# Pair attention in fp32: TensorE runs the first layer of two steps in a row, then two steps of scores

## The chip, the cores and the metric

The kernel runs on one core of a Trainium2 chip. The metric is the device time of one execution in microseconds (us), lower being better. Three executions of the kernel before gave 1324.63, 1326.22 and 1329.87 us, a median of 1326.22 us.

## What is computed

The reference takes x of shape 2048 x 40 x 64 (samples, fields, embedding). For every sample it forms all 780 products of two different fields, sends each through a small net (64 to 64, relu, 64 to 1), makes a softmax over the 780 logits and pools the products with it. All is fp32.

```
p = x[:, ROW, :]
q = x[:, COL, :]
inner = p * q
h = jax.nn.relu(jnp.einsum('bpe,he->bph', inner, W1) + b1)
logits = jnp.einsum('bph,oh->bpo', h, W2) + b2
attn = jax.nn.softmax(logits, axis=1)
pooled = jnp.sum(inner * attn, axis=1)
return pooled @ Wl.T + bl
```

## The kernel before

The samples are taken as two halves, whose embeddings lie above each other on the 128 partitions; a sample of the one half with its partner of the other is a "duo". One step (t) treats 2 duos, a round (r) is 16 steps, and 32 rounds make the whole. Each engine has its own program, and they meet in semaphores; there is no scheduler, so the order on an engine is the order in which its code calls the helpers.

One step goes through four engines' programs like this:

- VectorE (`products`, L463) multiplies fields pairwise into `inner`, a ring of 8 steps. Two steps share one small tail instruction (L482), after the odd step.
- TensorE (`hidden_layer`, L285) multiplies by W1. It does so in two halves, each into its own PSUM buffer (`h_bank[0]`, `h_bank[1]`), with 64x64 tiles of the array, so that four matmuls run at once (two row tiles, two column tiles). There is no second pair of such buffers: before it writes half 0 it waits until ScalarE has read half 0 of the step before (`hidden_ready`, L292), and the same for half 1. Half 0 also waits for the products.
- ScalarE (`relu`, L405) reads one half from PSUM, adds the bias, applies relu and writes `hidden`, a ring of 4 steps. Before step t it waits until step t-4 has been scored.
- TensorE (`score`, L303) multiplies `hidden` by w2 with 128x32 tiles, four at once, and adds 16 steps of a round into one of two logit banks. It waits for both relu halves of its step.

Between these, TensorE has other work that is not in every step: `turn_chunk` (L255, five transposes of new input, in steps 0 and 8 of a round) and `gram_matrix` (L266, sixteen small matmuls with 128x40 operands, in steps 4, 6, 12 and 14). Below, both are called fillers. ScalarE copies the results out of PSUM: `copy_turned` in steps 0, 0, 2, 3 and 8, 9, 11, 11 (parts 0 and 1 are the copies to `xt`, parts 2 and 3 those to `x_scaled`), and `copy_gram` in steps 5, 6, 13 and 15, always behind the two relus of that step. In step 3 it also computes the exponentials of the round before (`exp_of_round`). VectorE takes the maximum of the round before in step 7 of its own program (`softmax_of_round`, L488), after a wait for the last scores of that round, and its sums in step 8 (L500). In round 0 the places of chunk 1 are one step later, and round 31 has no work for a next round.

The order on TensorE is written in `round_steps` (L322): first layer of step t, scores of step t-1, then a filler if the step has one. The last scores of a round come in step 0 of the next.

Of the kernel before, what the change touches and what calls it, by code (L numbers as in the profile page):

```python
# [19 lines left out]
def pair_attention_kernel(nc, x, w1, b1, w2, b2, wl, bl, y):  # L20
# [17 lines left out]
    WINDOWS = 16  # L38
# [29 lines left out]
    with ExitStack() as ctx:  # L68
# [3 lines left out]
        def pb(name, shape):  # L72
            return ctx.enter_context(nc.psum_tensor(name, shape, F32))
# [44 lines left out]
        logit_bank = [pb(f"logit_bank{n}", [P, BANK]) for n in range(2)]  # L118
# [135 lines left out]
        def _(pe):  # L254
            def turn_chunk(r, c):  # L255

                pe.wait_ge(x_loaded[c], 32 * (r + 1))
                if not (r == 0 and c == 0):

                    pe.wait_ge(gram_copied, 2 * (r * CHUNKS_PER_ROUND + c))  # L260
                for t in range(TT):
                    last = nc.tensor.transpose(turn_bank[:, t * P:(t + 1) * P],  # L262
                                               x_rows[c][:, t, :, :].rearrange("p h e -> p (h e)"), ident[:, :])
                last.then_inc(turned, 1)

            def gram_matrix(r, c, part):  # L266

                pe.wait_ge(scaled_ready, 2 * (r * CHUNKS_PER_ROUND + c + 1))
                if not (r == 0 and c == 0 and part == 0):

                    pe.wait_ge(gram_copied, 2 * (r * CHUNKS_PER_ROUND + c) + part)
                for n in range(GRAM_DUOS):
                    duo = part * GRAM_DUOS + n
                    for half in range(2):
                        scaled_at = (2 * duo + half) * GRAM_COLUMNS
                        fields_at = duo * EXT + half * SPAN
                        last = nc.tensor.matmul(  # L277
                            turn_bank[half * TILE:half * TILE + GRAM_COLUMNS,
                                      GRAM_AT_COLUMN + n * FIELDS:GRAM_AT_COLUMN + (n + 1) * FIELDS],
                            x_scaled[:, scaled_at:scaled_at + GRAM_COLUMNS],  # L280
                            xt[c][:, fields_at:fields_at + FIELDS], start=True, stop=True,
                            tile_position=(0, half * TILE))
                last.then_inc(gram_ready, 1)

            def hidden_layer(r, t):  # L285
                for half in range(2):
                    if half == 0:

                        pe.wait_ge(inner_ready, inner_to(r, t))
                    if not (r == 0 and t == 0):  # L290

                        pe.wait_ge(hidden_ready, (r * WINDOWS + t) * 2 + half - 1)  # L292
                    for ab in range(2):
                        rows = slice(ab * EMBED, (ab + 1) * EMBED)
                        for j in range(STEP_DUOS):
                            at = (t % INNER_RING) * STEP + j * PAIRS + half * HALF
                            last = nc.tensor.matmul(  # L297
                                h_bank[half][j * TILE:(j + 1) * TILE, ab * BANK:ab * BANK + HALF],
                                w1_block[rows, rows], inner[rows, at:at + HALF], start=True, stop=True,
                                tile_position=(ab * TILE, j * TILE))  # L300
                    last.then_inc(h_ready, 1)

            def score(r, t, bank):  # L303

                pe.wait_ge(hidden_ready, (r * WINDOWS + t + 1) * STEP_DUOS)
                if t == 0 and r == 0:
                    pe.wait_ge(w2_loaded, 2 * 16)
                first = WINDOWS - 1 - t  # L310
                for half in range(2):
                    for ab in range(2):
                        g = 2 * half + ab
                        at = half * PAIRS + ab * HALF
                        last = nc.tensor.matmul(bank[g * QUAD:(g + 1) * QUAD, 0:HALF],  # L315
                                                w2_window[:, first:first + QUAD],
                                                hidden[t % RING][:, at:at + HALF],
                                                start=(t == 0), stop=(t == WINDOWS - 1),
                                                tile_position=(0, g * QUAD))
                last.then_inc(steps_scored, 1)  # L320

            def round_steps(r, odd, first=False, last=False):  # L322
                for t in range(WINDOWS):
                    hidden_layer(r, t)
                    if t:
                        score(r, t - 1, logit_bank[odd])
                    elif not first:
                        score(r - 1, WINDOWS - 1, logit_bank[1 - odd])
                    if first and t == 0:
                        gram_matrix(r, 0, 1)  # L330
                    for part in range(2):
                        if t == GRAM_AT[1][part] + first:
                            gram_matrix(r, 1, part)
                        if t == GRAM_AT[0][part] and not last:
                            gram_matrix(r + 1, 0, part)
                    if t == TURN_AT[1] + first:
                        turn_chunk(r, 1)
                    if t == TURN_AT[0] and not last:
                        turn_chunk(r + 1, 0)
# [7 lines left out]
            pe.wait_ge(w1_ready, 1)  # L347
            gram_matrix(0, 0, 0)
            round_steps(0, 0, first=True)
            for pair in range(ROUNDS // 2 - 1):  # L350
                round_steps(2 * pair + 1, 1)
                round_steps(2 * pair + 2, 0)
# [239 lines left out]
```

## Time and profile before

| | before |
|---|---|
| median of three executions | 1326.22 us |
| the profiled execution | 1324.93 us |
| its span (first to last instruction) | 1323.3 us |
| TensorE (PE) busy | 1306.2 us, 99% |
| ScalarE (ACT) busy | 1093.5 us, 83% |
| VectorE (DVE) busy | 1006.5 us, 76% |
| mean granted TensorE clock | 0.998 |

The rows of the trace further down are of this one execution. PE are TensorE's matmuls and PEld its weight loads. The ends of matmul records are modelled and overlap, so the pace of TensorE is read from the starts. An fp32 matmul of the program shows as two records.

### The profile page before, as it was taken

The page shows a single profiled execution, that of the slowest core. Times are in us where ns is not written, and L with a number is a line of the kernel's source. Part 1 is how long each engine was busy: PE and PEld are TensorE (multiplying, and loading weights), DVE is VectorE, ACT ScalarE, POOL GpSimd, SP SyncE. Part 2 cuts the span into 40 slices and gives each one's busy share as a digit, 9 for nine tenths or more (in the row PEclk, how much of TensorE's full clock was granted, in tenths as well). Part 3 has the DMA queues.
Part 4 walks back from the last instruction along what each step waited for, and adds up shares of the span by engine and source line. Part 5 has one row for each costly group of instructions (what it writes and reads, how often), then busy time and mean ns, then how long its engine had stood idle before and what let it go on. Part 6 is the DMA issues. An engine that isn't in the chain of part 4 may idle for free.

```text
span 1323.3 us, 38688 instructions
## 1 busy us (share of the span) xinstructions
PE 1306.2 (99%) x16709; PEld 463.4 (35%) x16709; DVE 1006.5 (76%) x1613; ACT 1093.5 (83%) x1475; POOL 0.7 (0%) x6
## 2 busy tenths in 40 slices
PE   7999999999999999999999999999999999999997
PEld 3333333333333333333333333333333333333332
DVE  8688777887777877778877778777787777887774
ACT  6888888888888888888888888888888888888885
POOL 0000000000000000000000000000000000000000
PEclk9999999999999999999999999999999999999999
DMA  2211211212112112111121121211211211112100
GB/s 48 47 36 40 47 24 40 47 30 47 37 28 46 34 44 47 21 43 38 39 46 24 41 46 30 47 42 23 46 34 43 46 22 43 36 40 46 24 21 20
DMA packets 176792, 49.73 MB, mean 38 GB/s; under 512 B 172528, under 2 KB 172528, under 8 KB 176624
## 3 DMA queue, kind: packets, MB, share of 16 engines
q1 hardware_dynamic: 176624, 47.26, 16.3%
q8 instruction: 133, 2.18, 0.7%
q14 instruction: 35, 0.29, 0.1%
HBM read 34.11 MB, written 13.12 MB: 36 GB/s over the span
## 4 chain that ended last, share of the span: by engine, by line
PE 98%; DVE 1%; ACT 0%; DMA 0%; issue 0%; SPq 0%; ACTq 0%
PE h_bank L297 57%; PE logit_bank L315 31%; PE turn_bank L277 7%; PE turn_bank L262 3%; DVE inner L474 0%; DMA x_rows<-in_r_x 0%; ACT hidden L410 0%; ACT xt L378 0%; DVE weighted L505 0%; ACT weight L418 0%; SPq L184 0%; PE turn_bank L359 0%; DVE row_max L491 0%; DVE part L564 0%; DVE inverse L568 0%
## 5 line engine op out<-in xcount | busy, mean ns | idle before, releaser
L410 ACT ACTIVATE hidden<-h_bank,b_col 128x780 f32<-128x780 f32 x1024 | 877.9, 909 | 178.2 <-PE h_bank L297 176.5
L474 DVE TENSOR_TENSOR inner<-xt 128x760 f32<-128x760 f32 x1024 | 908.5, 945 | 106.4 <-ACT xt L378 69.5
L297 PE MATMUL h_bank<-inner,w_block 64*64 64x390 f32 x8192 | 793.1, 501 | 0.7 <-DVE inner L482 0.7
L315 PE MATMUL logit_bank<-hidden,w_window 128*32 128x390 f32 x4096 | 441.8, 503 | 0.4 <-ACT hidden L410 0.4
L297 PEld LDWEIGHTS h_bank<-inner,w_block 64*64 64x64 f32 x8192 | 258.3, 132 | 409.3 <-ACT hidden L410 126.3
L315 PEld LDWEIGHTS logit_bank<-hidden,w_window 128*32 128x32 f32 x4096 | 80.7, 108 | 312.0 <-issue 310.9
L505 DVE CUSTOM_DVE_ANT_1 weighted<-weight,gram 128x380 f32<-128x380 f32 x32 | 27.7, 867 | 152.7 <-ACT weight L418 152.7
L277 PEld LDWEIGHTS turn_bank<-xt,x_scaled 128*40 128x40 f32 x4096 | 89.7, 123 | 84.2 <-issue 44.9
L277 PE MATMUL turn_bank<-xt,x_scaled 128*40 128x40 f32 x4096 | 104.9, 209 | 2.6 <-ACT x_scaled L390 2.6
L390 ACT ACTIVATE x_scaled<-turn_bank,wl_col 64x640 f32<-64x640 f32 x128 | 100.6, 786 | 1.6
L378 ACT COPY xt<-turn_bank 128x640 f32<-128x640 f32 (+1 forms) x128 | 68.3, 560 | 25.5 <-PE turn_bank L262 25.5
L401 ACT COPY gram_rows<-turn_bank 128x320 f32<-128x320 f32 x128 | 54.6, 426 | 14.5 <-PE turn_bank L277 14.5
L482 DVE TENSOR_TENSOR inner<-xt 128x80 f32<-128x80 f32 x256 | 60.2, 235 | 0.0
L491 DVE TENSOR_REDUCE row_max<-logit_bank 128x1 f32<-128x390 f32 x32 | 18.1, 564 | 49.0 <-PE logit_bank L315 49.0
L262 PE MATMUL turn_bank<-ident,x_rows 128*128 128x128 f32 x320 | 49.5, 286 | 4.6 <-DMA x_rows<-in_r_x 4.6
L262 PEld LDWEIGHTS turn_bank<-ident,x_rows 128*128 128x128 f32 x320 | 34.1, 141 | 44.6 <-issue 44.6
L418 ACT ACTIVATE weight<-logit_bank,exp_bias 128x390 f32<-128x390 f32 x32 | 18.8, 588 | 2.1 <-DVE exp_bias L497 2.1
L513 DVE CUSTOM_DVE_ANT_0 weighted<-weight,gram 64x10 f32<-64x10 f32 x64 | 10.8, 169 | 1.0
L493 DVE TENSOR_SCALAR round_stats<-row_max,b_col 128x1 f32<-128x1 f32 x32 | 6.9, 214 | 1.1
L497 DVE TENSOR_SCALAR exp_bias<-round_stats,b_col 128x1 f32<-128x1 f32 x32 | 6.8, 214 | 1.1
L418 ACT ACTIVATION_READ_ACCUMULATOR weight<-logit_bank,exp_bias 128x1 f32 x32 | 6.7, 209 | 0.0
L519 DVE COPY stats<-round_stats 128x4 f32<-128x4 f32 x32 | 5.5, 172 | 1.1
(28 smaller groups left out, 16.7 us busy)
## 6 DMA issues: line engine op xcount, KB each, us to landing
x_rows<-in_r_x SPq DMA_DIRECT2D x128, 160.0 KB, 3.4
gram_dram<-gram_rows SPq DMA_DIRECT2D x512, 25.0 KB
gram<-gram_dram SPq DMA_DIRECT2D x32, 400.0 KB, 3.3
w_rows<-in_L_rec_W SPq DMA_DIRECT2D x2, 16.0 KB, 2.3
wl_col<-in_L_rec_Wl SPq DMA_DIRECT2D x2, 0.2 KB, 2.3
b_col<-in_L_rec_b SPq DMA_DIRECT2D x2, 0.2 KB, 2.3
w_window<-in_L_rec_W SPq DMA_DIRECT2D x2, 0.2 KB, 2.3
b_col<-in_L_rec_b SPq DMA_DIRECT2D x1, 0.5 KB, 2.7
```

Source lines behind the costliest of these rows:

```text
L262: last = nc.tensor.transpose(turn_bank[:, t * P:(t + 1) * P], x_rows[c][:, t, :, :].rearrange("p h e -> p (h e)"), ident[:, :])
L277: last = nc.tensor.matmul(turn_bank[half * TILE:half * TILE + GRAM_COLUMNS, GRAM_AT_COLUMN + n * FIELDS:GRAM_AT_COLUMN + (n + 1) * FIELDS] ...
L297: last = nc.tensor.matmul(h_bank[half][j * TILE:(j + 1) * TILE, ab * BANK:ab * BANK + HALF], w1_block[rows, rows], inner[rows, at:at + HAL ...
L315: last = nc.tensor.matmul(bank[g * QUAD:(g + 1) * QUAD, 0:HALF], w2_window[:, first:first + QUAD], hidden[t % RING][:, at:at + HALF], star ...
L378: nc.scalar.copy(window_view(xt[c], at, [[EXT, CHUNK_DUOS], [TT, u], [1, TT]]), window_view(turn_bank, 0, [[U, CHUNK_DUOS], [1, u], [P, TT ...
L390: nc.scalar.activation(window_view(x_scaled, ab * SPAN, [[GRAM_COLUMNS, 2 * CHUNK_DUOS], [TT, U // 2], [1, TT]], rows), window_view(turn_b ...
L401: nc.scalar.copy(gram_rows[c][:, part * GRAM_DUOS:(part + 1) * GRAM_DUOS, :], turn_bank[:, GRAM_AT_COLUMN:GRAM_END].rearrange("p (d n) -> ...
L410: nc.scalar.activation(hidden[t % RING][:, half * PAIRS:(half + 1) * PAIRS].rearrange("p (a n) -> p a n", a=2), h_bank[half][:, :].rearran ...
L418: nc.scalar.activation(weight[:, :], bank[:, 0:HALF], ACT.Exp, bias=exp_bias[:, 0:1], accum_out=round_stats[:, 1:2]).then_inc(exp_done, 1)
L474: nc.vector.tensor_tensor(window_view(inner, to + half * HALF, [[PAIRS, STEP_DUOS], [SPAN, SHIFTS], [1, SPAN]]), window_view(xt[c], at + h ...
L482: nc.vector.tensor_tensor(window_view(inner, to + SHIFTS * SPAN, [[PAIRS, duos], [HALF, 2], [1, LAST]]), window_view(xt[c], at, [[EXT, duo ...
L505: nc.vector.tensor_tensor_reduce(out=weighted[:, 0:main].rearrange("p (d i) -> p d i", i=SPAN), in0=weight[:, 0:main].rearrange("p (d i) - ...
```

## The change

Only TensorE's order is changed. In an even step it runs the first layer (and the filler, if there is one) and no scores. In an odd step it runs the first layer and then the scores of the two preceding steps. The last step of a round is scored in step 1 of the next round, ahead of step 0. The last score of the whole kernel stays where it was.

```diff
             def round_steps(r, odd, first=False, last=False):
                 for t in range(WINDOWS):
                     hidden_layer(r, t)
-                    if t:
+                    if t % 2:
+
+                        if t > 1:
+                            score(r, t - 2, logit_bank[odd])
+                        elif not first:
+                            score(r - 1, WINDOWS - 1, logit_bank[1 - odd])
                         score(r, t - 1, logit_bank[odd])
-                    elif not first:
-                        score(r - 1, WINDOWS - 1, logit_bank[1 - odd])
                     if first and t == 0:
                         gram_matrix(r, 0, 1)
```

The next rows are TensorE's order of the kernel before in steps 2 to 5 of a round other than the first. L297 is the first layer (4 matmuls are one half of a step, the number of `h_bank` is the half), L315 is the scores, with the slot of the `hidden` ring that tells the step.

```order
L297 MATMUL h_bank0<-inner,w1_block 64x390 x4
L297 MATMUL h_bank1<-inner,w1_block 64x390 x4
L315 MATMUL logit_bank1<-hidden1,w2_window 32x390 x4
L297 MATMUL h_bank0<-inner,w1_block 64x390 x4
L297 MATMUL h_bank1<-inner,w1_block 64x390 x4
L315 MATMUL logit_bank1<-hidden2,w2_window 32x390 x4
L297 MATMUL h_bank0<-inner,w1_block 64x390 x4
L297 MATMUL h_bank1<-inner,w1_block 64x390 x4
L315 MATMUL logit_bank1<-hidden3,w2_window 32x390 x4
L277 MATMUL turn_bank<-xt1,x_scaled 40x40 x16
L297 MATMUL h_bank0<-inner,w1_block 64x390 x4
L297 MATMUL h_bank1<-inner,w1_block 64x390 x4
```

The same work in the changed kernel (an equal stretch, of a round with the other logit bank and chunk):

```order
L297 MATMUL h_bank0<-inner,w1_block 64x390 x4
L297 MATMUL h_bank1<-inner,w1_block 64x390 x4
L297 MATMUL h_bank0<-inner,w1_block 64x390 x4
L297 MATMUL h_bank1<-inner,w1_block 64x390 x4
L315 MATMUL logit_bank0<-hidden1,w2_window 32x390 x4
L315 MATMUL logit_bank0<-hidden2,w2_window 32x390 x4
L297 MATMUL h_bank0<-inner,w1_block 64x390 x4
L297 MATMUL h_bank1<-inner,w1_block 64x390 x4
L277 MATMUL turn_bank<-xt0,x_scaled 40x40 x16
L297 MATMUL h_bank0<-inner,w1_block 64x390 x4
L297 MATMUL h_bank1<-inner,w1_block 64x390 x4
L315 MATMUL logit_bank0<-hidden3,w2_window 32x390 x4
```

What moved: four halves of the first layer now follow each other where no filler stands, and a filler now stands between two first layers and no longer behind scores. The programs of the other engines are unchanged.

## Rows read from the trace of the kernel before

**Rows 1.** The page: busy time of the engines, and the chain that ended last, by engine.

```profile
PE 1306.2 (99%) x16709; PEld 463.4 (35%) x16709; DVE 1006.5 (76%) x1613; ACT 1093.5 (83%) x1475; POOL 0.7 (0%) x6
...
PE 98%; DVE 1%; ACT 0%; DMA 0%; issue 0%; SPq 0%; ACTq 0%
```

**Rows 2.** Timeline, TensorE: the six groups of four matmuls of one step (start, length).

```profile
609.86 0.56 PE L297 MATMUL h_bank<-inner,w_block 64*64 64x390 f32 x4
610.24 0.51 PE L297 MATMUL h_bank<-inner,w_block 64*64 64x390 f32 x4
610.57 0.51 PE L297 MATMUL h_bank<-inner,w_block 64*64 64x390 f32 x4
610.90 0.51 PE L297 MATMUL h_bank<-inner,w_block 64*64 64x390 f32 x4
611.34 0.54 PE L315 MATMUL logit_bank<-hidden,w_window 128*32 128x390 f32 x4
611.69 0.51 PE L315 MATMUL logit_bank<-hidden,w_window 128*32 128x390 f32 x4
```

**Rows 3.** Timeline, ScalarE, step 11, then 2 to 4: start, length, work [idle before].

```profile
610.88 1.72 ACT L410 ACTIVATE hidden<-h_bank,b_col 128x780 f32<-128x780 f32 x2 [0.55 <-PE h_bank L297]
612.48 1.60 ACT L390 ACTIVATE x_scaled<-turn_bank,wl_col 64x640 f32<-64x640 f32 x2
...
628.99 1.71 ACT L410 ACTIVATE hidden<-h_bank,b_col 128x780 f32<-128x780 f32 x2 [0.54 <-PE h_bank L297]
630.59 0.78 ACT L390 ACTIVATE x_scaled<-turn_bank,wl_col 64x640 f32<-64x640 f32 x1
631.27 1.70 ACT L410 ACTIVATE hidden<-h_bank,b_col 128x780 f32<-128x780 f32 x2
632.86 0.59 ACT L418 ACTIVATE weight<-logit_bank,exp_bias 128x390 f32<-128x390 f32 x1
...
633.56 0.79 ACT L390 ACTIVATE x_scaled<-turn_bank,wl_col 64x640 f32<-64x640 f32 x1
634.38 1.71 ACT L410 ACTIVATE hidden<-h_bank,b_col 128x780 f32<-128x780 f32 x2
```

**Rows 4.** Stretches (steps 2-3, 4-5, a round): length; busy PE, PEld, DVE, ACT, POOL; clock.

```profile
627.98:632.51 4.53, 4.53 (x53) 1.34 (x49) 0.70 (x1) 3.99 (x6) 0.00 (x0) 1.00 0.33 74
632.51:637.78 5.27, 5.27 (x84) 1.96 (x81) 4.14 (x12) 4.78 (x8) 0.00 (x0) 1.00 0.01 3
602.37:643.05 40.68, 40.68 (x526) 14.42 (x522) 31.30 (x51) 34.10 (x47) 0.00 (x0) 1.00 0.17 38
```

**Rows 5.** Timeline: where TensorE waited for a relu, in step 13 and at the end.

```profile
614.10 1.72 ACT L410 ACTIVATE hidden<-h_bank,b_col 128x780 f32<-128x780 f32 x2
...
615.87 0.21 PEld L297 LDWEIGHTS h_bank<-inner,w_block 64*64 64x64 f32 x8 [0.50 <-ACT hidden L410]
...
1311.36 1.71 ACT L410 ACTIVATE hidden<-h_bank,b_col 128x780 f32<-128x780 f32 x2 [0.55 <-PE h_bank L297]
...
1313.12 0.86 PE L315 MATMUL logit_bank<-hidden,w_window 128*32 128x390 f32 x8 [0.44 <-ACT hidden L410]
```

**Rows 6.** Timeline, TensorE: a gram and a turn, each with the first layer behind it.

```profile
599.37 0.81 PE L277 MATMUL turn_bank<-xt,x_scaled 128*40 128x40 f32 x32
...
600.11 1.54 PE L297 MATMUL h_bank<-inner,w_block 64*64 64x390 f32 x16
...
604.64 0.76 PE L262 MATMUL turn_bank<-ident,x_rows 128*128 128x128 f32 x5
...
605.33 1.54 PE L297 MATMUL h_bank<-inner,w_block 64*64 64x390 f32 x16
```

**Rows 7.** Timeline, VectorE: the softmax and the sums of one round.

```profile
625.15 0.56 DVE L491 TENSOR_REDUCE row_max<-logit_bank 128x1 f32<-128x390 f32 x1 [1.09 <-PE logit_bank L315]
...
633.57 0.87 DVE L505 CUSTOM_DVE_ANT_1 weighted<-weight,gram 128x380 f32<-128x380 f32 x1 [4.89 <-ACT weight L418]
```

**Rows 8.** Timeline, TensorE: the first layer of the kernel's first step.

```profile
10.75 2.88 PE L297 MATMUL h_bank<-inner,w_block 64*64 64x390 f32 x16 [0.68 <-DVE inner L482]
```

## The prediction

> **What bounds the kernel now.** I read the page first: TensorE is busy for 99% of the span, and 98% of the chain that ended last is TensorE's own work [rows 1]. So only TensorE's order and its waits can set the time. ScalarE has idle time, but it hands back the PSUM buffers, and must be followed step by step.
>
> Next I read TensorE's pace inside a step from the starts of its groups of four matmuls [rows 2]. They come 0.38, 0.33 and 0.33 us apart inside the first layer, 0.44 from the last one of it to the first of the scores, 0.35 inside the scores, and 0.44 from there to the next step, as two steps in 4.53 us [rows 4] tell: 4.53/2 less the 1.83 between the first and last start of the step. The bare pace is thus 0.33. A change between first layer and scores, which use different tile shapes, costs 0.11 more, and the group after it 0.02 to 0.05 more. That is the price which this change saves.
>
> Then the two clocks of a step. With the start of a first layer as zero, ScalarE's first relu starts at 1.01 (628.99 against 627.98) and the two take 1.71 together, so they end at 1.92 and 2.72 (one takes 0.91, the second starts 0.80 after the first) [rows 3, 4]. Where TensorE really waited for a relu, its next work began 0.05 behind the relu's end: 1313.12 after 1311.36 + 1.71, and 615.87 after 614.10 + 1.72 [rows 5]. Today the scores (0.79) stand in that interval and hide it nearly everywhere.
>
> **Steps 2-3 and 10-11 (no filler).** Here the next first layer could follow at 1.04 + 0.33 = 1.37, but half 0 of the PSUM buffer is read until 1.92. With its two waits it starts at about 2.0, and its second group 0.38 later, as after any fresh start. Half 1 needs the second relu: 2.72 + 0.05 = 2.78 with rounding. Then 0.38 to its second group (3.16), 0.44 to the scores (3.60). The scores of two steps are four groups, 0.35 + 0.33 + 0.33 + 0.44 = 1.45 to the next first layer. The pair takes 5.05 us instead of 4.53 [rows 4]: **0.52 more**. Of the two changes of shape saved here, one only makes the wait longer, and the other is lost in it.
>
> **Steps with a filler between.** In the pairs 0-1, 4-5, 6-7, 8-9, 12-13 and 14-15 the turn or gram, which stood behind scores, now stands between the two first layers. The trace has no filler behind a first layer. The nearest rows are the changes to another shape on either side of scores, 0.44 both, so I take 0.44: filler at 1.48. A gram holds TensorE for 0.74 until the next first layer and a turn for 0.69 [rows 6], so that starts at 2.22 or 2.17. The first relu was done at 1.92 and the second (2.72 + 0.05) is wanted at 2.22 + 0.71 = 2.93: the filler hides both waits. What remains is the gain: scores of two steps cost 1.45 in one run and 2 x 0.79 = 1.58 apart, **0.13 less**. The join of two score runs is the unknown. Its bounds are the 0.33 of an undisturbed join and the 0.44 of a change of shape [rows 2]; it is the same shape on the same bank, with weights that change at every group anyway, so I take 0.33. At 0.35 it would add 0.02 x 256 pairs = 5 us.
>
> Here a rule speaks. The Trainium skill (TensorEngine Tiling, Key Properties) says that a change of tiling mode drains the array, and its page TensorE: Matmul & The Clock Gate (Step-by-step) gives a drain as about 128 cycles, 0.05 us at 2.4 GHz as an estimate. The rows show 0.11, twice that. By the page's figure, half of the 0.11 would be something else that could stay with the join of two runs of scores, at 0.39; this is a rival below.
>
> **Where ScalarE comes late.** Its copies now meet relus that come in other intervals. In pair 2-3, after the relus of step 2, `x_scaled` starts at 1.01 + 1.60 = 2.61, the relus of step 3 at +0.82 = 3.43, the exponentials 1.59 later (5.02), the second `x_scaled` at 5.72, and the relus of step 4 at 6.54 [rows 3]. They end at 7.45 and 8.25. TensorE starts step 4 at 5.05, wants the gram at 6.53 (its input is there at about 6.6), and step 5 at 7.34, which waits until about 7.56; half 1 comes at 8.30. With 0.38 + 0.44 + 1.45 behind it pair 4-5 takes 5.51 where 5.27 stood [rows 4]: **0.24 more**. In pair 10-11 the relus of step 11 start at 3.03 and two `x_scaled` 1.60 behind that, for 1.60 [rows 3], until 6.21. The relus of step 12 end at about 7.14 and 7.94, half 1 of step 13 wants 7.98 and gets 7.99: pair 12-13 saves only **0.06**. After steps 0 and 8 the copies to `xt` push relus by 0.3, but the next first layer has more slack than that (its relu ends at 4.4, wanted at 5.1).
>
> **Costed at nothing.** The relu ring: step t waits for the scores of step t-4, and these are still done a pair earlier. VectorE takes the round's maximum about 2 us later, since the last scores of a round now follow step 1; but it then waits 4.89 us for the exponentials anyway [rows 7], and these stand on ScalarE behind step 3, some 4 us after the later maximum. The DMAs wait for turns and gram copies, a round ahead of their use. Before the first step of a pair, its products: VectorE is busy 76% [rows 1] and loses nothing.
>
> **Sum.** Per round: 2 x 0.52 - 4 x 0.13 + 0.24 - 0.06 = 0.70 us, so 41.4 instead of 40.68. Thirty such rounds: 21.0. Round 0 has fillers one step later, so four plain pairs (2, 4, 6, 10), one pair unchanged and three filled: 4 x 0.52 - 2 x 0.13 - 0.06 = 1.8. Round 31 has no fillers in its second half: 4 x 0.52 + 0.24 - 2 x 0.13 = 2.1, and the last pair, whose final scores follow without the 0.44 us wait of [rows 5], saves 0.1, so 2.0. In all 24.8 us. The profiled execution took 1324.93, which gives 1349.7; it lies 1.3 below the median of 1326.22, against which I forecast **1351.0 us**, 1.9% slower. A measurement of this kernel tells 0.5% (6.6 us) from no change.
>
> **Rivals.**
> - ScalarE comes late in one more filled pair per round, as in pair 4-5. That costs 0.37 x 32 = 12, so 1363 us. For it: ScalarE is busy 83%, and in pair 12-13 the margin is nil. Chance 0.10.
> - The join of two score runs costs 0.39: 0.06 x 256 = 15, so 1366 us. Against it: the other joins of one shape show 0.33. Chance 0.04.
> - The waits are worse than hidden. If fillers did not cover the relus, 192 filled pairs would cost 0.65 more each, so 1476 us. Or the clock drops: in the first step of the kernel, at 1.2 GHz, a first layer is 2.88 us long [rows 8] against 1.54 at 2.4 GHz [rows 6]; if the eight groups after each of 64 waits went at that pace, 2.7 us each, that is 1524 us. Against it: the wait is near 0.7 us, and after the one of 0.44 at the end TensorE goes on at full pace. Together 0.04. The Trainium skill (TensorE: Matmul & The Clock Gate, A second HAM failure mode) describes such clock swings from short idle times between groups; no idle of this kind is in the trace before.
> - **Faster.** The fillers leave the array cheaper behind a first layer than behind scores, on both sides: 0.11 less before and 0.11 less after. That is 192 x 0.22 = 42 us, so 1309 us. It decides from 0.13 per filled pair on, where 192 pairs make up for the 24.8. For it: nothing in the trace shows a filler behind a first layer. Against it: the changes that it does show, into scores and out of them, cost 0.44 alike, and a filler's tiles are of another shape than a first layer's, too. Chance 0.05.
> - Nearly no change: only one of these two sides is cheaper, 192 x 0.11 = 21, so 1330 us. Chance 0.07.
>
> **How the numbers follow.** My forecast has 0.70. Its own bounds: joins at 0.35 add 5; waits in pair 4-5 and after the relus that cost nothing extra take off 8 to 13. The range of 1338 to 1363 holds this and the first rival, 0.80 in all. Slower by over 0.5%: 0.70 + 0.10 + 0.04 + 0.04 = 0.88; within: 0.07; faster: 0.05.
>
> **What would show it.** In the profile after, TensorE's idle time in front of a first layer should be named as a wait for ScalarE's relus, some 0.6 us in each of two pairs per round, with a round of about 41.4 us. Scores should come in runs of four groups, 0.35, 0.33, 0.33 apart. Pairs 0-1, 6-7, 8-9 and 14-15 should be 0.13 shorter than before and plain ones 0.5 longer. It is wrong if filled pairs gain more than 0.13 or plain ones lose less than 0.4, or if VectorE's products become what a first layer waits for.

## The result and the profile after

| | before | after |
|---|---|---|
| median of four executions | 1325.45 us | 1344.55 us (1344.09 to 1344.99) |
| the profiled execution | 1324.93 us | 1344.98 us |
| its span | 1323.3 us | 1343.4 us |
| TensorE busy | 1306.2 us, 99% | 1285.1 us, 96% |
| ScalarE busy | 1093.5 us, 83% | 1079.8 us, 80% |
| mean granted TensorE clock | 0.998 | 0.998 |

The changed kernel is slower by 1.4%: the ratio of its runs to those of before is 1.0143, 95% interval 1.0128 to 1.0158. The forecast was 1351.0 us, in a range from 1338 to 1363. The direction and the mechanism were right; the loss is 19 to 20 us where 24.8 were worked out.

From the page after, the busy times and the chain that ended last (for [rows 1]):

```profile
PE 1285.1 (96%) x16709; PEld 482.9 (36%) x16709; DVE 1006.3 (75%) x1613; ACT 1079.8 (80%) x1475; POOL 0.7 (0%) x6
...
PE 80%; ACT 12%; DVE 5%; issue 2%; DMA 0%; ACTq 0%; SPq 0%; DVEq 0%
```

TensorE is busy 21 us less by its records (the saved changes of shape are part of that) and yet ends 20 us later. The chain, which was 98% TensorE, now has a part through ScalarE (12%, mostly its relus) and VectorE (5%; what that name is worth is told below).

The stretches of one round after, two steps each, then the whole round (columns as in [rows 4]: length, busy PE, PEld, DVE, ACT, POOL, granted clock, DMA share, GB/s). The order is steps 0-1, 2-3, and so on:

```profile
426.81:431.89 5.08, 5.08 (x57) 1.92 (x53) 1.16 (x3) 4.19 (x7) 0.00 (x0) 1.00 0.29 53
431.89:436.94 5.05, 4.52 (x53) 1.38 (x49) 2.20 (x5) 4.20 (x7) 0.00 (x0) 1.00 0.24 55
436.94:442.32 5.38, 5.26 (x85) 2.07 (x81) 4.77 (x12) 4.98 (x8) 0.00 (x0) 1.00 0.00 2
442.32:447.45 5.13, 5.13 (x84) 2.13 (x80) 5.13 (x8) 3.80 (x6) 0.00 (x0) 1.00 0.10 19
447.45:452.54 5.09, 5.09 (x57) 1.92 (x53) 4.05 (x7) 4.07 (x6) 0.00 (x0) 1.00 0.45 116
452.54:457.58 5.04, 4.51 (x52) 1.38 (x48) 4.86 (x7) 3.83 (x6) 0.00 (x0) 1.00 0.26 59
457.58:462.87 5.29, 5.26 (x84) 2.07 (x81) 5.29 (x8) 4.89 (x7) 0.00 (x0) 1.00 0.00 0
462.87:468.01 5.14, 5.14 (x85) 2.14 (x81) 3.85 (x6) 3.68 (x6) 0.00 (x0) 1.00 0.01 3
426.81:468.01 41.20, 40.00 (x527) 15.02 (x523) 31.31 (x51) 33.65 (x47) 0.00 (x0) 1.00 0.17 38
```

Two stretches of before that the prediction's rows do not show, pairs 0-1 and 12-13 of a round:

```profile
419.34:424.56 5.22, 5.22 (x57) 1.86 (x53) 3.40 (x8) 4.64 (x8) 0.00 (x0) 1.00 0.23 39
449.40:454.75 5.35, 5.35 (x85) 1.96 (x81) 5.35 (x8) 4.95 (x7) 0.00 (x0) 1.00 0.00 0
```

The plain pairs, those without a filler (second and sixth row after), are 5.04 to 5.05 us long with 0.53 us in which TensorE does nothing by its records; before they had 4.53 and no idle time. Pairs 0-1 and 8-9 have gone from 5.22 to 5.09, pairs 6-7 and 14-15 from 5.27 to 5.13. Pair 4-5 has gone from 5.27 to 5.38, pair 12-13 from 5.35 to 5.29. A round is 41.20 instead of 40.68.

The timeline of a plain pair and the step after it, TensorE and ScalarE alone (for [rows 3]; start, length, work, idle before it and what ended it):

```profile
596.72 1.54 PE L297 MATMUL h_bank<-inner,w_block 64*64 64x390 f32 x16
...
597.73 1.71 ACT L413 ACTIVATE hidden<-h_bank,b_col 128x780 f32<-128x780 f32 x2 [0.85 <-PE h_bank L297]
598.75 0.24 PEld L297 LDWEIGHTS h_bank<-inner,w_block 64*64 64x64 f32 x8 [1.18 <-DVE inner L477]
598.78 1.60 PE L297 MATMUL h_bank<-inner,w_block 64*64 64x390 f32 x16 [0.53 <-ACT hidden L413]
599.33 0.78 ACT L393 ACTIVATE x_scaled<-turn_bank,wl_col 64x640 f32<-64x640 f32 x1
599.49 0.21 PEld L297 LDWEIGHTS h_bank<-inner,w_block 64*64 64x64 f32 x8 [0.50 <-ACT hidden L413]
600.01 1.70 ACT L413 ACTIVATE hidden<-h_bank,b_col 128x780 f32<-128x780 f32 x2
...
600.31 1.52 PE L315 MATMUL logit_bank<-hidden,w_window 128*32 128x390 f32 x16
...
601.76 1.54 PE L297 MATMUL h_bank<-inner,w_block 64*64 64x390 f32 x16
...
602.29 0.79 ACT L393 ACTIVATE x_scaled<-turn_bank,wl_col 64x640 f32<-64x640 f32 x1
...
603.11 1.72 ACT L413 ACTIVATE hidden<-h_bank,b_col 128x780 f32<-128x780 f32 x2
```

The second first layer starts at 598.78, that is 2.06 behind the first (worked out: "about 2.0"). The first relu ended at 597.73 + 0.91 = 598.64. Its half 1 gets its weights at 599.49, 0.05 behind the end of the second relu at 599.44. That is also where it would be without a second wait (598.78 + 0.38 + 0.33), so the two relus bind together here. The scores start at 3.59 (worked out: 3.60).

The row of the weight load names VectorE as what ended the wait, and over the whole trace about half of these waits go by that name:

```profile
PE h_bank L297 <- ACT hidden L413: 19.7, 38, 0.5
PE h_bank L297 <- DVE inner L477: 17.1, 32, 0.8
```

The prediction had set this as a sign of being wrong, so it needs an answer. A wait for two semaphores is put down to one of them by the profile. In pair 2-3 VectorE had taken the round's maximum at 596.20, which in its program stands behind the products of step 7, so those of step 3 had long been done. In pair 10-11 it had begun on the next round at 617.55, while step 11 waited until 619.44. That wait ended 0.12 to 0.15 behind the first relu's end (618.38 + 0.91 = 619.29), as in pair 2-3 (0.11 to 0.14). In experiment 1 the profile names the relus 63 times and VectorE once for the same waits. The name is the profile's choice; the waits are for the relus.

The groups of four matmuls of the scores, one by one (for [rows 2]):

```profile
600.31 0.54 PE L315 MATMUL logit_bank<-hidden,w_window 128*32 128x390 f32 x4
600.66 0.51 PE L315 MATMUL logit_bank<-hidden,w_window 128*32 128x390 f32 x4
600.99 0.51 PE L315 MATMUL logit_bank<-hidden,w_window 128*32 128x390 f32 x4
601.32 0.51 PE L315 MATMUL logit_bank<-hidden,w_window 128*32 128x390 f32 x4
```

They come 0.35, 0.33 and 0.33 apart and 0.44 later the next shape starts, as worked out. The join of two steps' scores costs nothing.

### The profile page after: what moved, and what is told of

The parts are those of the page before. It is cut to its first block, busy times and chain, and to the rows that moved or that the text cites. A ratio compares the mean times of both kernels' runs of the same rounds, so it can differ in the third digit from the quotient of the medians.

```text
span 1343.4 us, 38688 instructions
## 1 busy us (share of the span) xinstructions
PE 1285.1 (96%) x16709; PEld 482.9 (36%) x16709; DVE 1006.3 (75%) x1613; ACT 1079.8 (80%) x1475; POOL 0.7 (0%) x6
## 4 chain that ended last, share of the span: by engine, by line
PE 80%; ACT 12%; DVE 5%; issue 2%; DMA 0%; ACTq 0%; SPq 0%; DVEq 0%
PE h_bank L297 47%; PE logit_bank L315 24%; ACT hidden L413 10%; PE turn_bank L277 7%; DVE inner L477 5%; ACT xt L381 2%; PE turn_bank L262 2%; DMA x_rows<-in_r_x 0%; ACT weight L421 0%; DVE row_max L494 0%; ACTq L412 0%; DVE weighted L508 0%; SPq L184 0%; PE turn_bank L362 0%; ACT x_scaled L393 0%
## 5 line engine op out<-in xcount | busy, mean ns | idle before, releaser
L297 PE MATMUL h_bank<-inner,w_block 64*64 64x390 f32 x8192 | 799.1, 504 | 42.0 <-ACT hidden L413 19.7
L297 PEld LDWEIGHTS h_bank<-inner,w_block 64*64 64x64 f32 x8192 | 251.6, 132 | 469.7 <-issue 182.9
L315 PE MATMUL logit_bank<-hidden,w_window 128*32 128x390 f32 x4096 | 388.6, 497 | 0.0
L315 PEld LDWEIGHTS logit_bank<-hidden,w_window 128*32 128x32 f32 x4096 | 106.9, 109 | 257.0 <-issue 256.4
```

Of the source, the lines that this page charges most:

```text
L297: last = nc.tensor.matmul(h_bank[half][j * TILE:(j + 1) * TILE, ab * BANK:ab * BANK + HALF], w1_block[rows, rows], inner[rows, at:at + HAL ...
```

## The experiments

My theory: the loss is the wait of the second first layer for the relus, only in the two plain pairs of a round, with a smaller part in pair 4-5 where ScalarE is late; each filled pair gains the price of one change of shape. The first rival: something else in the new order (later scores, ScalarE late in all pairs) makes the loss. All versions use the same small edit of TensorE's order, with a list of the pairs that are changed (by their even step; with all eight it is the changed kernel's order):

```diff
+            waiting = []
...
-                    if t % 2:
-
-                        if t > 1:
-                            score(r, t - 2, logit_bank[odd])
-                        elif not first:
-                            score(r - 1, WINDOWS - 1, logit_bank[1 - odd])
-                        score(r, t - 1, logit_bank[odd])
+                    if t not in PAIRED:
+                        for scored in waiting:
+                            score(*scored)
+                        waiting.clear()
+                    waiting.append((r, t, logit_bank[odd]))
```

**1. Only the plain pairs.** `PAIRED = [2, 10]`.

> Only the pairs without a filler (steps 2-3 and 10-11) run two first layers in a row; all others keep the order of before. Theory (the loss is the wait for the two relus in just these pairs): both go from 4.53 to 5.04 us, all others stay, a round takes 41.7 us, total 1358 us against 1325. Rival (the loss comes from the later scores in all pairs, or from a ScalarE that is late everywhere): a quarter of the change's loss, about 1330 us.

Measured: 1355.46 us (1354.98 to 1356.24), ratio to before 1.0228, interval 1.0212 to 1.0243. A plain pair, a filled pair behind it, and the round:

```profile
434.10:439.15 5.05, 4.52 (x53) 1.38 (x49) 0.71 (x1) 4.51 (x7) 0.00 (x0) 1.00 0.30 68
439.15:444.42 5.27, 5.27 (x84) 2.04 (x81) 4.67 (x12) 4.26 (x7) 0.00 (x0) 1.00 0.01 2
...
428.88:470.50 41.62, 40.57 (x526) 14.64 (x522) 31.39 (x51) 34.04 (x47) 0.00 (x0) 1.00 0.17 37
```

Two pairs of eight cost 30 us by themselves, more than the whole change. All other pairs stay at 5.22 and 5.27; pair 12-13 even falls from 5.35 to 5.27, probably since a longer pair 10-11 lets ScalarE catch up. The theory that the loss sits in these pairs stands; the rival falls.

**2. Only the filled pairs.** `PAIRED = [0, 4, 6, 8, 12, 14]`.

> The reverse: all six pairs with a filler are changed, the two plain pairs keep the order of before. Rival (each filled pair saves 0.13 whatever its neighbours are): a round of 39.9 us, total about 1299 us. Theory (x_scaled copies of ScalarE come too late for a gram that no scores stand in front of, once the plain pairs no longer hold TensorE back): pairs 0-1, 6-7, 8-9, 14-15 save 0.14 each, but 4-5 and 12-13 take about 5.9 and 6.0 instead of 5.27 and 5.35, a round of 41.4 us, total about 1348 us. The wait then shows in front of the gram.

Measured: 1350.05 us (1349.48 to 1350.40), ratio 1.0186, interval 1.0169 to 1.0203. Taking away the two pairs that carry the loss makes the kernel slower than the full change. Pairs 0-1, 6-7, 8-9 and 14-15 are 5.09 and 5.13 long; 4-5 takes 5.89 and 12-13 takes 6.00. The timeline of steps 3 to 5:

```profile
437.43 1.54 PE L298 MATMUL h_bank<-inner,w_block 64*64 64x390 f32 x16
...
438.48 0.79 ACT L394 ACTIVATE x_scaled<-turn_bank,wl_col 64x640 f32<-64x640 f32 x1
...
439.29 1.71 ACT L414 ACTIVATE hidden<-h_bank,b_col 128x780 f32<-128x780 f32 x2
...
439.32 0.81 PE L278 MATMUL turn_bank<-xt,x_scaled 128*40 128x40 f32 x32 [0.35 <-ACT x_scaled L394]
440.35 1.60 PE L298 MATMUL h_bank<-inner,w_block 64*64 64x390 f32 x16 [0.22 <-ACT hidden L414]
```

The gram could have run at 437.43 + 1.48 = 438.91, but its input `x_scaled` is there at 439.27. And the relus of step 4 start behind that copy, at 439.29, so that the first layer of step 5 waits too. In the old order, the scores of step 3 stood ahead of the gram and hid this; in the full change the slow pair 2-3 did, since ScalarE used its wait to catch up. The two losses thus do not add: the waits of the plain pairs hide one that would be there without them.

**3. Only the four pairs without this conflict.** `PAIRED = [0, 6, 8, 14]`.

> Only pairs 0-1, 6-7, 8-9, 14-15 are changed (a filler covers the relus, and no x_scaled copy is due). Theory: each saves 0.14 us, the other four stay: a round of 40.13 us, total 1308 us, faster than both kernels. Rival (the changed order costs something in every pair that the wait view does not show): more than 1315 us.

Measured: 1309.49 us (1309.15 to 1309.79), ratio 0.9880, interval 0.9865 to 0.9895. A round takes 40.13 us: the four pairs are at 5.09 and 5.13, the rest as before. It beats both kernels. Run again beside a later version it took 1309.36 us (1309.33 to 1309.55):

> The version with pairs 0-1, 6-7, 8-9 and 14-15 changed, once more beside the version above on the same chip: 1309.5 us by every theory; it tells whether the two differ.

**4. Shorter relus.** The changed kernel, with relus over a part of the columns; `hidden` is zeroed once at the start. This kernel leaves 180 of the 780 pairs out of the net, so its time is of use and its output is not:

```diff
-                    hidden[t % RING][:, half * PAIRS:(half + 1) * PAIRS].rearrange("p (a n) -> p a n", a=2),
-                    h_bank[half][:, :].rearrange("p (a n) -> p a n", a=2)[:, :, 0:HALF],
+                    hidden[t % RING][:, half * PAIRS:(half + 1) * PAIRS].rearrange("p (a n) -> p a n", a=2)[:, :, 0:RELU],
+                    h_bank[half][:, :].rearrange("p (a n) -> p a n", a=2)[:, :, 0:RELU],
```

> The changed kernel with relus that treat only the first 300 of each 390 columns (the other 90 of hidden stay zero, so those pairs are left out of the net). ScalarE's relu should take 0.72 instead of 0.91 us, TensorE's work is the same. Theory (the length of the relus sets the wait): plain pairs 4.77 instead of 5.04, pairs 4-5 and 12-13 at 5.13, a round of 40.3 us, total about 1316 us. Rival (the wait is a fixed cost of the restart or of the semaphores): plain pairs stay at 5.04, total above 1338 us.

Measured: 1322.94 us (1321.93 to 1323.69), 21.6 us less than the changed kernel. From the groups and the stretches (a plain pair, pair 4-5, the round):

```profile
L415 ACT ACTIVATE hidden<-h_bank,b_col 128x600 f32<-128x600 f32 x1024 | 724.7, 761 | 365.9 <-PE h_bank L299 362.5
```

```profile
427.73:432.57 4.84, 4.46 (x53) 1.48 (x49) 2.19 (x5) 3.83 (x7) 0.00 (x0) 1.00 0.21 48
432.57:437.70 5.13, 5.13 (x84) 2.14 (x81) 4.92 (x13) 4.04 (x8) 0.00 (x0) 1.00 0.01 2
...
422.64:463.04 40.40, 39.65 (x527) 15.48 (x523) 31.31 (x51) 28.98 (x46) 0.00 (x0) 1.00 0.17 39
```

A relu of 600 elements takes 0.76 us, not the 0.72 that I had worked out, and the plain pair 4.84 instead of 4.77. The wait follows the length of the relus. With the first relu 0.15 us shorter, the second first layer starts at 1.91 (429.64 - 427.73) instead of 2.06. The other 0.05 of the 0.20 is half 1, which no longer waits for the second relu: its second group comes 0.33 behind its first (430.32, 430.65) and not 0.38 (599.49, 599.87). Pairs 4-5 and 12-13 are at 5.13, so their waits are gone as well, as ScalarE is no longer late.

The total flatters the old order a little: the zeroing holds up the first transposes, and the first layer of the kernel starts at 15.54 instead of 10.96, 4.6 us late. With that taken off, this version would take about 1318 us by my estimate, 0.5% less than the old order with its full relus; as measured it is 0.2% less (ratio 0.9982, interval 0.9972 to 0.9991).

**5 to 7. ScalarE's copies earlier.** If pairs 4-5 and 12-13 are long only because `x_scaled` is late, copies one step earlier should free them:

```diff
-        TURN_COPY_AT = [[8, 9, 11, 11], [0, 0, 2, 3]]
+        TURN_COPY_AT = [[8, 8, 9, 10], [0, 0, 1, 2]]
...
-        EXP_AT = 3
+        EXP_AT = 4
```

With the six filled pairs changed:

> The six filled pairs changed and the plain ones not, as in the second experiment, but ScalarE's copies come earlier: parts 1 to 3 of copy_turned in steps 8, 9, 10 and 0, 1, 2 (before: 9, 11, 11 and 0, 2, 3), the exponentials one step later (4). Theory (what made pairs 4-5 and 12-13 long was only the late x_scaled): these two fall from 5.9 and 6.0 to 5.13, a round of 39.8 us, total 1299 us, faster than every other version. Rival (these pairs are long for another reason, or the moved copies hit other relus): above 1309 us.

With the old order on TensorE:

> The same moved copies and exponentials with TensorE's order of before. Theory (TensorE bounds that order and waits only 0.07 per round in pair 12-13): pair 12-13 goes from 5.35 to 5.27, a round of 40.6 us, total 1323 us, within 0.3% of before. Rival (the earlier copies alone bring the gain of the experiment beside it): about 1300 us.

With all eight pairs changed:

> The changed kernel (all eight pairs) with the moved copies. Theory: pairs 4-5 and 12-13 at 5.13 instead of 5.39 and 5.28, the plain pairs still at 5.04: a round of 40.8 us, total 1332 us, still slower than before; so the plain pairs alone, not ScalarE's late copies, make the change a loss. Rival (the late copies are the loss): below 1325 us.

| | total us | ratio to before (95%) | round us | pair 2-3 | pair 4-5 | pair 12-13 |
|---|---|---|---|---|---|---|
| six pairs | 1308.45 | 0.9875 (0.9860 to 0.9890) | 40.07 | 4.62 | 5.19 | 5.18 |
| old order | 1331.49 | 1.0048 (1.0035 to 1.0061) | 40.89 | 4.62 | 5.33 | 5.32 |
| all pairs | 1331.54 | 1.0048 (1.0034 to 1.0061) | 40.80 | 5.04 | 5.14 | 5.13 |

The third is as expected: with ScalarE's lateness taken away, the plain pairs still make the change a loss. The first gained 42 us on the second experiment, so the late copies were the cause there, but it missed 1299 by 9 us. And the second went against my expectation: in the old order these copies cost 6 us. In both, pairs 2-3 and 10-11 have 0.09 more, and pairs 4-5 and 12-13 have 0.05 more than they could, for half 1 of their first layer waits too. In the first version the copy behind the relus of step 2 starts at 422.60 and ends at 423.39; the first relu of step 3 starts at 423.42 and ends at 424.33, and step 4's first layer, due at 424.38, comes at 424.47. An unpaired step leaves ScalarE 0.54 us idle [rows 3], less than one such copy. Yet a copy stood behind the relus of step 2 before, too, and delayed those of step 3 by 0.02 only; experiments 8 and 9 show the difference between the two.

**8. Only one `x_scaled` copy taken ahead**, in the filled pair, where there is room: `[[8, 8, 9, 11], [0, 0, 1, 3]]`, with the six filled pairs changed and the exponentials in step 4.

> The six filled pairs changed, the plain ones not, with only one x_scaled copy taken ahead: copy_turned in steps 8, 8, 9, 11 and 0, 0, 1, 3, exponentials in step 4. Theory (the version with two copies ahead lost its gain because an x_scaled behind the relus of step 2 or 10 delays the relus of the next step, and with them the first layer of step 4 or 12): pairs 2-3 and 10-11 at 4.53 instead of 4.62, pairs 4-5 and 12-13 at 5.14 instead of 5.19, a round of 39.8 us, total about 1300 us. Rival (that gain does not exist): 1308 us or more.

Measured: 1311.77 us (1311.41 to 1312.62), ratio 0.9897, interval 0.9882 to 0.9912. Pair 2-3 is at 4.53 again, as said, but 4-5 at 5.33 and 12-13 at 5.34, so this misses by 12 us. It is also 2.4 us slower than the four changed pairs of experiment 3 run beside it (1309.36): the two further pairs bring nothing here. ScalarE's timeline in steps 3 and 4 says why:

```profile
424.56 1.71 ACT L414 ACTIVATE hidden<-h_bank,b_col 128x780 f32<-128x780 f32 x2 [0.55 <-PE h_bank L298]
426.30 0.79 ACT L394 ACTIVATE x_scaled<-turn_bank,wl_col 64x640 f32<-64x640 f32 x1
427.12 1.72 ACT L414 ACTIVATE hidden<-h_bank,b_col 128x780 f32<-128x780 f32 x2
```

The copy starts 0.03 behind the end of the relus (426.27), and the next relu 0.03 behind the copy's end (427.09). Other neighbours on ScalarE overlap: two relus of 0.91 take 1.71. In this version, as in the old order, the `x_scaled` copy in this place is the one of partitions 64 to 127.

**9. The two copies exchanged**, the one of the upper partitions first (the edit is against experiment 8; the wait for the last gram stays with whichever copy comes first):

```diff
-        TURN_COPY_AT = [[8, 8, 9, 11], [0, 0, 1, 3]]
+        TURN_COPY_AT = [[8, 8, 11, 9], [0, 0, 3, 1]]
...
-                    elif part == 2:
+                    elif part == 3:
```

> As the version before it, but of the two x_scaled copies the one for partitions 64 to 127 goes first (step 1 and 9) and the one for partitions 0 to 63 second (step 3 and 11). Theory (in every trace so far the copy of the upper partitions starts 0.025 us behind its neighbour's end and is followed so, while all others overlap their neighbours by 0.1 us; this kept the relus of step 4 late by 0.14 to 0.28): the second copy overlaps again, pairs 4-5 and 12-13 take 5.14 instead of 5.33, a round of 39.8 us, total about 1300 us. Rival (the gap belongs to whatever copy comes second, or to the missing wait): 5.33 again, 1311 us.

Measured: **1299.10 us** (1298.86 to 1300.10), ratio 0.9806, interval 0.9793 to 0.9820. ScalarE around both copies, then pair 4-5 and the round:

```profile
414.96 1.75 ACT L414 ACTIVATE hidden<-h_bank,b_col 128x780 f32<-128x780 f32 x2
416.73 0.79 ACT L394 ACTIVATE x_scaled<-turn_bank,wl_col 64x640 f32<-64x640 f32 x1
417.55 1.72 ACT L414 ACTIVATE hidden<-h_bank,b_col 128x780 f32<-128x780 f32 x2
419.82 1.71 ACT L414 ACTIVATE hidden<-h_bank,b_col 128x780 f32<-128x780 f32 x2 [0.55 <-PE h_bank L298]
421.42 0.78 ACT L394 ACTIVATE x_scaled<-turn_bank,wl_col 64x640 f32<-64x640 f32 x1
422.10 1.70 ACT L414 ACTIVATE hidden<-h_bank,b_col 128x780 f32<-128x780 f32 x2
```

```profile
421.07:426.21 5.14, 5.14 (x85) 2.14 (x81) 1.75 (x8) 5.14 (x9) 0.00 (x0) 1.00 0.00 0
...
411.45:451.23 39.78, 39.78 (x526) 15.06 (x523) 31.05 (x51) 33.50 (x47) 0.00 (x0) 1.00 0.18 39
```

The upper copy (416.73) still starts behind its neighbour's end, now where there is room. The lower one (421.42) starts 0.11 before the end of the relus, and the next relu 0.10 before its own end. TensorE is busy without a gap for the whole round, and every filled pair has its 0.13 to 0.14. This is the best version: 1.9% faster than before and 3.4% faster than the change. Since the wait for the gram has moved to the upper copy and the gap is still there, that wait is not what makes it.

**10. The same copies with the old order.**

> The same copies and exponentials, with TensorE's order of before. Theory (that order is bound by TensorE, only pair 12-13 gains its 0.07 us): 40.6 us per round, total about 1323 us, so that the gain of the version beside it is the order's. Rival (the gain is the copies'): 1300 us.

Measured: 1333.02 us (1331.78 to 1333.25), ratio 1.0058, interval 1.0044 to 1.0071. The expected 1323 was wrong: pairs 2-3 and 10-11 take 4.69 instead of 4.53, because the copy of step 1 or 9 pushes the relus of the next step (in pair 2-3, the first layer of step 3 comes at 430.11 where 430.00 was due, and its half 1 waits too). In the new order the scores of two steps stand behind the first layer of step 1 and give that copy its room. The 34 us between this and the version before it are the order's: of 1.14 us per round (40.92 to 39.78), six filled pairs give 0.82 and this room 0.32. In the old order the copies alone cost 8 us.

## Why the prediction held, and where it was off

**Plain pairs.** Right: 5.05 worked out, 5.04 to 5.05 measured. Experiment 1 shows that the loss sits in these pairs, experiment 4 that its size follows the relus. The first layer started at 2.06 where "about 2.0" was said; this did no harm, since half 1 waited for the second relu until 2.77 (2.78 worked out) in any case.

**Filled pairs.** Right: turn and gram hide both waits, and the saving is 0.14 (5.22 to 5.09, 5.27 to 5.13) where 0.13 was said; that is over the prediction's own limit by 0.01, which is the rounding of its terms. The change from a first layer to a filler costs 0.44, as from scores: in the changed kernel the last group of the first layer starts at 602.79 and the gram at 603.23. A filler that left the array cheaper on either side would have made the saving 0.24 or more. So neither of the two rivals with a cheaper filler had anything to it.

**The join of scores.** Right: 0.33. The Trainium skill (TensorEngine Tiling, Key Properties) says that a change of tiling mode drains the array; by that rule, the trace agrees, since the extra 0.11 appears at changes of shape and not at the join. Its drain of about 128 cycles (TensorE: Matmul & The Clock Gate, Step-by-step), 0.05 us as an estimate, is half of what a change costs here; the other half did not stay with the join, so a change costs 0.11 as a whole.

**Pair 4-5.** This is the term that was mis-sized: "0.24 more" by the prediction, 0.11 to 0.12 measured, about 0.13 x 31 rounds = 4 us. The step that failed is "the relus of step 3 at +0.82 = 3.43". They started at 600.01 - 596.72 = 3.29. I had used for both `x_scaled` copies the 0.82 that lies between the second one and the relus behind it; the row of the first in [rows 3] shows 0.68 (630.59 to 631.27). So the relus of step 4 came at 6.39 instead of 6.54, and the gram did not wait at all. What is left of the loss is step 5: its half 1 got its weights at 8.16 (604.88), where 8.30 had been worked out. It is the same difference between lower and upper copy that experiments 8 and 9 made visible; it stood in the rows already.

**Pair 12-13.** The saving of 0.06 came out, by luck. Its base was not 5.27: in the old order this pair took 5.35, with waits that one row of [rows 5] had shown. Nor was its end 5.21: it took 5.29, since the relus of step 12 started at 6.30 (623.67 - 617.37) where 6.21 had been worked out. Two errors of 0.08 cancel.

**The sum.** In the profiled executions: rounds 1 to 30 grew by 15.5 us (21.0 worked out: 4 of the difference is pair 4-5, the rest is rounding in eight pairs), round 31 by 1.8 (2.0), round 0 by 2.6 (1.8) and the start by 0.2. The surplus of round 0 is none of the change's steps: its seven pairs after the first grew by 1.7 together. The kernel's first matmuls run at half pace, and in the run after this lasted longer. The first layers of steps 0 and 1 in the timeline after (for [rows 8]):

```profile
10.96 2.88 PE L297 MATMUL h_bank<-inner,w_block 64*64 64x390 f32 x16 [0.67 <-DVE inner L485]
...
14.98 2.40 PE L297 MATMUL h_bank<-inner,w_block 64*64 64x390 f32 x16
```

Step 1 takes 2.40 us there, while before it took 1.54 from 14.78 on, the usual length: 0.86 us. In the versions pair 0-1 of round 0 took from 6.5 to 7.8 us, and the one kernel of experiment 3 took 6.63 in one trace and 7.38 in the other, so it varies by itself. The prediction spoke of 1.2 GHz there; the granted clock of that stretch reads 1.00 in both traces, so these rows show the half pace and not its cause, and the prediction's 1.2 GHz is not shown here.

**The rivals.** ScalarE late in one more pair: no, in the change it was less late than worked out, but experiment 2 shows how near it was: without the plain pairs' waits, pairs 4-5 and 12-13 lose 0.62 and 0.65 us. A lower clock after the waits: the granted clock is 1.00 in all pairs, and the groups after a wait keep their 0.33. The Trainium skill (TensorE: Matmul & The Clock Gate, A second HAM failure mode) describes clock swings for short idle times between groups; with idle times of 0.53 us by the records, twice in 41 us, this trace shows none.

## What to carry to other kernels

Running work of one shape in a row saves the changes between shapes (0.11 us each here), but what stood between two uses of a buffer also hid the time in which another engine empties it; before merging, check for each place what else covers that time, and merge only there. Here two of eight places cost more than the other six gave, and the selective order with matching copies was 1.9% faster where the uniform one was 1.4% slower. A wait that is removed can be the one that let a busy engine catch up, so try parts of a change both alone and together.

## What the runs showed of the hardware

ScalarE's `x_scaled` copy from PSUM over partitions 64 to 127 does not overlap with the instruction before it or behind it (it starts 0.02 to 0.03 us after the end of the one, and the next follows it 0.02 to 0.04 behind its own end), while the same copy over partitions 0 to 63 and two relus in a row overlap by about 0.10, in most places. It goes with the copy and not with its place in the program or its wait: in the traces of experiments 8 and 9 all 63 of these copies inside the rounds show it, on both sides. In a chain that is otherwise dense this took 0.2 us off pair 4-5 (5.33 to 5.14). What causes it was not tried, and no other instruction of this kernel that ScalarE runs in the rounds is over the upper partitions alone, so it is not shown that the partitions are the reason.
